# Down products of two expert pairs in one group, in both mixture-of-experts layers

## The reference

```python
# layer 0, on the normalised x, with D = 64, H = 256, E = 8 experts, K = 2
gate_scores = jnp.einsum('bsd,ed->bse', x, Wg) + bg
topk_scores, topk_idx = jax.lax.top_k(gate_scores, K)
topk_probs = jax.nn.softmax(topk_scores, axis=-1)
combine = jnp.sum(topk_probs[..., None] * jax.nn.one_hot(topk_idx, E, dtype=x.dtype), axis=-2)
for e in range(E):
    h = jax.nn.relu(jnp.einsum('bsd,hd->bsh', x, W1[e]) + b1[e])
    y = jnp.einsum('bsh,dh->bsd', h, W2[e]) + b2[e]
    out = out + combine[..., e:e + 1] * y
# layer 1, on flat = rmsnorm(x), hidden width 170
for e in range(E):
    hh = jax.nn.silu(flat @ w1[e].T) * (flat @ w3[e].T)
    out = out + weights[:, e:e + 1] * (hh @ w2[e].T)
```

## Time and profile before

| | |
|---|---|
| three runs, us | 1102.91, 1093.0, 1104.26; median 1102.91 |
| profiled execution | 1097.99 us, span of the core 1096.2 us |
| mean granted TensorE clock | 0.987 of full speed |
| busy, share of the span | PE 92%, PEld 66%, DVE 74%, ACT 53%, POOL 36% |
| `up` products, line 1579, both layers | 322.6 + 294.1 us, 1976 of them |
| down products, line 1594, both layers | 118.7 + 118.6 us, 1600 records |
| evictions, lines 1225, 1489 (layer 0), 1220, 1483 (layer 1) | 149.6, 56.8, 123.9, 131.3 us |
| a tile's period, from one turn of the shares to the next | layer 0: 303.06 to 324.87, 21.81 us; layer 1: 893.48 to 919.08, 25.60 us |
| weighing, lines 1444, 1446 | 44.0 + 41.0 us, 100 of them |

### The profile page before, as it was taken

One profiled execution on the slowest core, in us unless ns is written; L12 is line 12 of the kernel. 1 busy time (PEld: TensorE's weight loads), 2 busy tenths in 40 slices (PEclk: granted clock), 3 DMA queues, 4 the chain that ended last, 5 costly groups with the idle time before them and its releaser, 6 DMA issues. The chain is left out here.

```text
span 1096.2 us, 23392 instructions
## 1 busy us (share of the span) xinstructions
PE 1004.6 (92%) x8389; PEld 720.9 (66%) x8389; DVE 808.0 (74%) x1982; ACT 580.6 (53%) x1331; POOL 399.7 (36%) x391
## 2 busy tenths in 40 slices
PE   5798889879999999998988799988999999999997
PEld 2476766557677767775765577755777777777774
DVE  2595968967766776777777589866877778777775
ACT  2275646565565656564338666765444444444441
POOL 3233602312433343333357568710133333333333
PEclk9899999999999999999999989999999999999999
DMA  8300000003223222322001000000122221221122
GB/s 227 136 2 1 2 2 1 1 12 87 49 51 82 66 50 51 84 63 50 1 19 49 7 2 2 2 3 0 51 65 71 71 65 55 56 55 56 55 56 68
DMA packets 76423, 50.16 MB, mean 46 GB/s; under 512 B 4196, under 2 KB 75124, under 8 KB 75924
## 3 DMA queue, kind: packets, MB, share of 16 engines
q1 hardware_dynamic: 75972, 44.59, 15.8%
q0 software_dynamic: 336, 4.07, 0.9%
HBM read 45.99 MB, written 2.66 MB: 44 GB/s over the span
## 5 line engine op out<-in xcount | busy, mean ns | idle before, releaser
L1579 PE MATMUL moe_psU<-moe_nT_parts,moe_w_hi 128*128 128x320 f32 x988 | 322.6, 338 | 14.1 <-DVE moe_hid L1483 8.8
L1579 PE MATMUL moe_psU<-moe_nT_parts,moe_w_lo 128*128 128x320 f32 x988 | 294.1, 308 | 0.0
L1579 PEld LDWEIGHTS moe_psU<-moe_nT_parts,moe_w_hi 128*128 128x128 f32 x988 | 185.6, 188 | 71.7 <-issue 42.4
L1225 ACT ACTIVATE moe_hid<-moe_psU,middle 128x320 f32<-128x320 f32 x312 | 149.6, 528 | 99.3 <-PE moe_psU L1579 97.7
L1220 ACT ACTIVATE moe_silu<-moe_psU 128x320 f32<-128x320 f32 x286 | 123.9, 439 | 139.2 <-PE moe_psU L1579 112.1
L1579 PEld LDWEIGHTS moe_psU<-moe_nT_parts,moe_w_lo 128*128 128x128 f32 x988 | 186.3, 189 | 0.7 <-issue 0.7
L1483 DVE TENSOR_TENSOR moe_hid<-moe_psU,moe_silu 128x320 f32<-128x320 f32 x286 | 131.3, 485 | 34.4 <-ACT moe_silu L1220 27.6
L1111 POOL TENSOR_TENSOR moe_y_sum<-moe_y_sum,moe_y 128x320 f32<-128x320 f32 x96 | 81.7, 872 | 145.7 <-DVE moe_y L1444 82.1
L1594 PE MATMUL moe_psY<-moe_hid,late 128*64 128x320 f32 x800 | 118.7, 439 | 0.0
L1594 PE MATMUL moe_psY<-moe_hid,middle 128*64 128x320 f32 x800 | 118.6, 439 | 0.0
L139 POOL TENSOR_TENSOR moe_stats<-moe_stats,minus_half 128x5 f32<-128x5 f32 x26 | 30.5, 1171 | 186.3 <-DVE moe_stats L1326 186.3
(11 more groups left out here) (367 smaller groups left out, 1901.3 us busy)
## 6 DMA issues: line engine op xcount, KB each, us to landing
moe_share<-shares SPq DMA_DIRECT2D x208, 160.0 KB, 4.5
images<-in_x SPq DMA_DIRECT2D x8, 576.0 KB, 11.4
late<-in_late POOLq DMA_DIRECT2D x1, 2263.5 KB, 11.3
out_tokens<-h SPq DMA_DIRECT2D x13, 160.0 KB, 1.8
middle<-in_middle POOLq DMA_DIRECT2D x1, 1554.0 KB, 7.1
project_turns<-in_turns SPq DMA_DIRECT2D x8, 160.0 KB, 2.2
early<-in_early SPq DMA_DIRECT2D x1, 1043.0 KB, 18.9
turns_first<-in_turns SPq DMA_DIRECT2D x4, 160.0 KB, 2.3
```

The costliest lines, as they stand in the source:

```text
L1225: act.activation(hid[hid_of(g, u)][:, :], psU[u % 4][:, 0:HALF], ACT.Relu, bias=late[:, c["b1"]][:, k:k + 1]).then_inc(hid_act, 1)
L1579: last = pe.matmul(psum[:, 0:HALF], w[:, col:col + SPLIT], moving, start=(part == 0), stop=(part == 1))
```

## The change

- `down_two` puts the down products of pairs p and p + 1 in one group, at the places (0,4) and (2,4) of layer 0 and (0,1) and (2,1) of layer 1 (DOWNS), where `down` stood once in each pair. The first pair is reported when the second's first part is issued.
- psY becomes three banks: an even pair's 640 columns at 128, an odd pair's at 768, the turned shares at 1408. A product covers 384 or 256 columns; a `hid` buffer holds both halves.
- For that, layer 0's psM shrinks from two banks to one, and its transposes and turned outputs go in two parts (4 and 1 positions) as layer 1's; layer 1's gate banks go from three to two.
- `weigh` of the first pair stands at the group's place, that of the second behind the eviction of the next unit (`late_pair`). Before a group TensorE waits for the copy of the turned shares too (`shares_set`).
- VectorE takes 12 of layer 0's 32 evictions instead of 8. The places of shares, transposes and VectorE's small steps are set anew in both layers.

```diff
     if layer == 0:
-        on_dve = [(u - first_of[units[u][0]]) in (2, 6) for u in range(UPG)]
-        gate_bank = None
+        on_dve = [(u - 5) % 16 in (0, 3, 6, 9, 12, 14) for u in range(UPG)]
+        silu_of = None
     else:
         on_dve = [True] * UPG
...
-        psU = [ps(f"psU{k}", 128, HALF) for k in range(4 if layer == 0 else 5)]
-        psY_both = ps("psY", 128, 1024)
-        psY = psY_both[:, :].rearrange("p (x n) -> p x n", x=2)[:, :, 0:HALF]
-        MBANKS = 2 - layer
-        psM = ps("psM", 128, MBANKS * 512)
-        LOGITS_AT = TOK if layer == 0 else 128
-        SHARES_AT = LOGITS_AT + 2 * T * E
+        psU = [ps(f"psU{k}", 128, HALF) for k in range(4)]
+        psY = ps("psY", 128, 1536)
+        EVEN_AT, ODD_AT, SHARES_AT = 128, 768, 1408
+        psM = ps("psM", 128, 512)
+        LOGITS_AT = 128
...
         def outputs_ps(p, last):
 
-            if last and p % 2:
-                return [psU[half][:, 0:HALF] for half in range(2)]
-            return [psY[:, half, :] for half in range(2)]
+            if last and p == 2:
+                return [(half * HALF, (half + 1) * HALF, psU[half][:, 0:HALF]) for half in range(2)]
+            at, middle = (ODD_AT, 2 * B) if p % 2 and not last or p == 1 else (EVEN_AT, 3 * B)
+            return [(0, middle, psY[:, at:at + middle]), (middle, TOK, psY[:, at + middle:at + TOK])]
 
...
+        OUTS, READS = [(1, 0), (1, 3)], [(1, 1), (1, 4)]
         if layer == 0:
-            LOGITS, DOWN = (0, 2), 4
-            OUTS, READS = [(1, 0)], [(1, 1)]
-            SHARES, SHARES_READ = (2, 6), (2, 7)
-            TURN, KEEP = [(3, 2)], [(3, 2)]
-            HI, EXP = (1, 5), (2, 3)
+            LOGITS, DOWNS = (0, 2), [(0, 4), (2, 4)]
+            SHARES, SHARES_READ = (3, 6), (3, 7)
+            TURN, KEEP = [(3, 2), (3, 4)], [(3, 2), (3, 4)]
+            HI, EXP = (2, 4), (2, 5)
             NORM_STEPS, ASK_STEPS, END_STEPS = 5, TOP_TWO_LINKS + 1, 5
-            LAST_SLOTS = {(0, 7): "ss", (1, 1): "sssss", (1, 7): "sssss", (2, 1): "mmm", (2, 7): "mmm", (3, 3): "s"}
-            SLOTS = {(0, 4): "aaaannnn", (1, 0): "n", (1, 2): "n", (1, 4): "aaaaan", (1, 7): "aa", (2, 1): "aaa", (2, 4): "neeeeee"}
+            LAST_SLOTS = {(0, 7): "ss", (1, 1): "sssss", (1, 7): "sssss", (3, 0): "mmm", (3, 2): "mmm", (3, 5): "s"}
+            SLOTS = {(0, 4): "nnnnnnaaa", (1, 0): "aa", (1, 3): "aa", (1, 6): "a", (2, 4): "naaaaaan",
+                     (2, 7): "ee", (3, 1): "ee", (3, 3): "ee"}
         else:
-            LOGITS, DOWN = (0, 0), 1
-            OUTS, READS = [(1, 0), (1, 3)], [(1, 1), (1, 4)]
+            LOGITS, DOWNS = (0, 0), [(0, 1), (2, 1)]
             SHARES, SHARES_READ = (3, 0), (3, 0)
             TURN, KEEP = [(3, 1), (3, 3)], [(3, 1), (3, 3)]
             HI, EXP = (1, 3), (0, 3)
             NORM_STEPS, ASK_STEPS, END_STEPS = 2, 2, 18
-            SLOTS = {(0, 1): "aaaannn", (0, 4): "ee", (1, 1): "neeeeeee", (1, 4): "eee", (2, 1): "neeeeeee"}
+            SLOTS = {(0, 1): "aaaannneeeeee", (1, 1): "ne", (1, 4): "ee", (2, 1): "neeeeeeeeeee"}
 
...
+                    late_pair = None
                     for p, k, u in places():
                         evict(g, u)
+                        if late_pair is not None:
+                            weigh(g - 1, late_pair)
+                            late_pair = None
                         for kind in SLOTS.get((p, k), "") + (LAST_SLOTS.get((p, k), "") if ahead and not front else ""):
                             if kind in work:
                                 next(work[kind], None)
-                        if g and k == DOWN:
+                        if g and (p, k) in DOWNS:
                             weigh(g - 1, p)
+                            late_pair = p + 1
...
-                        turns = [(psU[u % 2], 0, up_mm), (psU[2 + gate_bank[u]], 1, gate_mm)]
+                        turns = [(psU[u % 2], 0, up_mm), (psU[2 + u % 2], 1, gate_mm)]
                     for psum, kind, done in turns:
                         if kind == 1:
-                            before = [v for v in range(u) if gate_bank[v] == gate_bank[u]]
-                            wait_evicted(pe, g, before[-1] if before else
-                                         max(v for v in range(UPG) if gate_bank[v] == gate_bank[u]) - UPG)
+                            wait_evicted(pe, g, u - 2)
...
+                def down_two(j, p):
+
+                    need(pe, weighed, j * PAIRS + p)
+                    pe.wait_ge(shares_set, j + 1)
+                    down_ready(j, p + 1)
+                    down_part(j, p, 0)
+                    down_part(j, p, 1)
+                    down_part(j, p + 1, 0).then_inc(down_mm, 1)
+                    down_part(j, p + 1, 1).then_inc(down_mm, 1)
+
+                def down_last(j, p):
+
+                    if p == 3:
+                        pe.wait_ge(weighed, j * PAIRS + 2)
+                    down_ready(j, 3)
+                    down_part(j, p, 0, True)
+                    down_part(j, p, 1, True).then_inc(down_mm, 1)
 
...
-                    need(pe, out_read, (g - 1) * PARTS)
-                    pe.transpose(psM[0:T * E, SHARES_AT:SHARES_AT + B],
+                    need(pe, weighed, g * PAIRS)
+                    pe.transpose(psY[0:T * E, SHARES_AT:SHARES_AT + B],
...
-                        if g and k == DOWN:
-                            down(g - 1, p)
-                        elif layer == 0 and k == DOWN and p < 3:
-                            products_unread(pe, psY_both[:, 0:512], early, ec, 1)
+                        if g and (p, k) in DOWNS:
+                            down_two(g - 1, p)
+                        elif layer == 0 and k == 4 and p < 3:
```

110 lines of the change are left out of this document (53 added, 57 removed).

## The result

| | before | after |
|---|---|---|
| median of the runs, us | 1102.55 (1093.0 to 1104.26, 4 runs) | 1156.03 (1151.41 to 1156.39, 4 runs) |
| ratio | | 1.0494, 95% interval 1.0428 to 1.056 |
| profiled execution: span, mean granted clock | 1096.2 us, 0.987 | 1153.9 us, 0.977 |
| from the start to layer 0's first unit | 226.2 us | 228.1 us |
| layer 0's expert stage, to the recurrence's first transpose | 300.6 us | 338.0 us |

The changed kernel is 4.9% slower, and the forecast, 1116 within 1094 to 1130, was too low. So both expert stages have to be explained, layer 0 first.

The account below looks back on a forecast made before the run. TensorE was taken to bound the kernel, VectorE next at 78%. Layer 0's +17.8 us and layer 1's 0 gave +18 on the profiled 1097.99, so 1116 us, range 1094 to 1130.

Parts of the forecast that it names:

- the group of 32 records in 4.46 us: Sign to check: two pairs' down products back to back take TensorE 4.46 us; at 4.6 the gain is gone.
- the gain of a merge: Both layers: merging two lone groups of down products saves 0.34 us, two merges a tile, -16.3 us in all.
- The unread product: Layer 0 at (1,4): an unread 128x512 product now runs in every tile, +0.86 a tile, +10.3 us over 12 tiles.
- The wait for the turned outputs: Layer 0, behind unit (1,3): part 1 waits until ScalarE has copied part 0 out of the shared bank, 0.63.
- for the transposes: Layer 0, behind (3,4): part 1 of the transposes waits for the copy of part 0, +0.32.
- Layer 1's waits for VectorE: Layer 1, two gate banks: +0.56 behind the first group, +0.45 at the second, +0.4 at (1,1) and (1,4) together.
- the shares' wait: Layer 0, step "Shares": late share DMAs delay VectorE's weighing and eviction; TensorE waits 0.4 for the bank, between 0 and 1.5.
- I take 0.85 for both together: Layer 0: turned-outputs wait 0.63 and shares' wait 0.4 lie within 2 us and partly swallow each other, so 0.85.
- Times 11.5 (the last tile turns less): Layer 0's sum: +1.55 a tile over 11.5 tiles gives +17.8 us.
- Layer 1: ... = 0.0 a tile: Layer 1's sum: -0.68 - 0.71 + 0.56 + 0.45 + 0.4, so no change a tile.
- "Worse", 1125: Rival: GpSimd's adds hold up VectorE's routing steps, up to 0.8 a tile in layer 1, +9 us; chance 18%.
- VectorE's four more evictions: Layer 0: some 0.5 each, in VectorE's idle windows, costed at nothing; without that cover 0.2 a tile.

Follow-up runs that it names:

- e12: Kernel before, with TensorE made to wait for eviction behind units (2,0), (2,1) and (2,2) of layer 0; ratio 1.0361 to the kernel before.
- e2: Changed kernel with layer 1's expert stage as before, layer 0's as changed; ratio 1.0339 to the kernel before.
- e3: Changed kernel with the unread 128x512 product in the first tile of layer 0 only; ratio 1.0384 to the kernel before.
- e5: Changed kernel with layer 0's shares turned at (3,1) instead of (3,6), routing steps moved ahead for it; ratio 1.0391 to the kernel before.
- e9: Changed layer 0 with unread product in first tile only, shares at (3,2), two-part turns apart, small steps re-placed; layer 1 as before; ratio 1.0006 to the kernel before.
- e7: Changed kernel with VectorE's small steps spread over units in each layer's first tile and layer 0's last; ratio 1.0461 to the kernel before.
- e11: Kernel before with two gate banks instead of three in layer 1, nothing grouped; ratio 1.0226 to the kernel before.
- e1: Changed kernel with layer 0's expert stage as before, layer 1's as changed; ratio 1.0115 to the kernel before.
- e10: Layer 0 as before, layer 1 as changed with the shares turned at (3,1) instead of (3,0); ratio 1.0186 to the kernel before.

## Why the prediction was wrong

**Right.** What bounds the kernel; the group of 32 records in 4.46 us; the gain of a merge: by the forecast's own count, with the slow steps on both sides, a lone group costs 2.49 and a double one 4.65, so a tile gains 0.66 against 0.68. (From the product before to the product behind, four lone groups take 10.17 us and two double ones 9.40; but of these 0.77 two ordinary steps of 0.15 are not saved, they only stand elsewhere.) The unread product, 0.80 against 0.86. The wait for the turned outputs, 0.76 against 0.63, and for the transposes, 0.37 against 0.32. Layer 1's waits for VectorE: 0.44 behind the first group, 0.31 ahead of the second, 0.36 in small ones and 0.35 at the shares, 1.46 together against 1.41, though not where I put them. On the shares' wait the walk itself was good: it had VectorE's eviction end 6.6 into the group, and TensorE gets the bank at 6.66 (330.28). Its upper bound was too low by its own steps: a landing of 5.9 gives 1.8, not 1.5.

**Wrong in layer 0, per tile.** The step "Shares" had VectorE wait for the DMA and then TensorE for 0.4, and "I take 0.85 for both together". The two came out as 0.57 and 0.76, added in full: 1.33. And the step did not ask what the turned shares themselves wait for: `end_routing`'s last steps had moved to (3,3), and one of them lasts 0.83 beside GpSimd's add, so `routed` came 0.54 late. Down to the rows the tile is -0.66 + 0.80 + 0.76 + 0.57 + 0.37 + 0.54 = 2.38, less 0.2 for two steps from one turned piece to the next that fall away in the splits. Its period says 24.05 - 21.84 = 2.21, the forecast 1.55. Eleven such tiles are 24.3 us instead of 17.1: 7.2 of the 19.6 that are missing.

**Wrong in layer 0, the clock.** The forecast had no term for it: it took TensorE's waits at their length. The eleven tiles sum to 271.1 against 240.1 before, 6.7 more than eleven times 2.21. Two of them, 26.32 and 26.73, in which the clock fell, are 5.0 of it; why others at a clock of 1.00 take up to 24.7 I do not know. e12 shows that waits alone can do this to the clock, and e2, e3 and e5 that like waits need not. So a part of the 4.9% differs from execution to execution.

**Wrong in layer 0, the ends.** "Times 11.5 (the last tile turns less)" took the first tile as free and the last as half of 1.55. The first is nearly free, 0.4. The last tile and what follows it cost 6.0, against 0.8: TensorE stands there for 1.31 for the routing weights, 1.14 for an eviction and 0.60 and 0.77 for copies of turned outputs, and the clock is at 0.96. The last tile's steps for the recurrence were moved as well. e9, in which they and the shares have other places, is at 42.1 there; which of the moves did it was not tried by itself.

**Wrong in layer 1.** The waits' sum was right; what failed is "Layer 1: ... = 0.0 a tile", by what it left out. Each short wait also makes the step behind it slow: 16 of a tile's 44 steps from the high to the low product take 0.22 to 0.26 instead of 0.15, where 11 did before: +0.50. Where the slow steps are counted by themselves, the groups give 0.77 less the two ordinary steps, 0.47. The tile is -0.47 - 0.71 + 1.46 + 0.50 = 0.78 by these, 0.79 by its period. Ten such tiles make 7.9 us. The first tile, which the forecast took as free, costs 5.5, the second 1.9, the last 1.0: together 16.3. In the first the bursts of small steps have lost their cover and the clock is at 0.87; e7 took 3.0 of it out.

**The rivals.** "Worse", 1125, had the right place for its mechanism and the wrong layer for its price: GpSimd's adds hold VectorE's steps (e11 shows it at its clearest), but in the changed kernel this adds 0.54 in layer 0 rather than 0.8 in layer 1. The range ended at 1130 because it bounded the terms of the sum only: it had none for the clock, for layer 1's first tile or for the slow steps behind its waits, and too small a one for layer 0's end. VectorE's four more evictions, costed at nothing, were not tried by themselves.

## What to carry to other kernels

A change that gives away PSUM banks is priced by what the banks did for the engines behind TensorE: two gate banks instead of three cost 23 us alone, where layer 1's merges give 8. Where a group is moved, look in the tables at everything that hid under it, in the first and the last tile too, and at what the moved step itself waits for. Waits of TensorE on one cause surface one behind the other, so taking out the first moves it; find the DMA or the engine that is late. And short waits cost more than their length: 0.1 for each slow step behind them, and at times the clock.

## What was not expected of the hardware

- Three waits of 0.62 to 0.94 us within 4 us brought the granted clock down in every third of otherwise equal tiles, for 1.6 us a time (e12). In e5 a tile with waits of 0.60, 0.31 and 0.32, farther apart, kept it at 1.00 in ten tiles of ten. One code, in two executions, lost it in two ordinary tiles (after) and in none (e2).
- A `tensor_scalar` of 40 elements with one SBUF input took 0.88 us beside a GpSimd add (e11, line 1418), as long as one with two.
- A stage at the full clock repeats itself closely beside other code: layer 0 of the kernel before took 300.6 us in before, e1, e10 and e11. The changed layer 0, with its waits, did so in its sum only: 337.0 and 338.0, with parts that differ by 1.6 to 4.6 us.
